# A graph attention layer on one core: the running maximum moves from TensorE to VectorE, the accumulator update one group later, and the end is reordered

## The chip, the core and the metric

The kernel runs on one core of a Trainium2 chip. TensorE (PE) multiplies matrices out of SBUF into PSUM, VectorE (DVE) and ScalarE (ACT) work element by element, GpSimd (POOL) here does nothing but issue indirect gathers, and SyncE (SP) issues the other transfers. The engines run side by side and are ordered by semaphores alone. The metric is the device time of one execution in microseconds. The kernel before takes 2543.44 us (median of three runs, 2543.19 to 2546.44).

## The reference

One message passing layer over 6250 nodes and 206,250 edges that are sorted by their receiver `dst`, all in float32:

```python
h = maximum(layernorm(x), 0)
m = concat(h[src], h[dst], edge_attr)               # 64 + 64 + 32 columns
messages = silu(m @ W1 + b1) @ W2 + b2
att = softmax(silu(m @ Wa1 + ba1) @ Wa2 + ba2)      # over all edges at once
agg = segment_sum(messages * att, dst)
out = x + silu(concat(h, agg) @ Wu1 + bu1) @ Wu2 + bu2
```

The softmax runs over all edges, so the kernel keeps a running maximum and rescales what it has summed whenever the maximum grows.

## The kernel before, in words

**Preparation.** For all nodes the kernel writes two tables to memory: `p_tab`, the part of the two first layers that comes from the source node (128 columns), and `q_tab`, the part from the receiver.

**The groups.** The edges are cut into 81 groups: 80 of 20 tiles of 128 edges, and a last one (number 80, `LAST`) of 12 tiles. Because receivers are sorted, the receivers of a group lie in a window of 96 nodes. Each group is handled in quarters of 4 tiles (five quarters, three in the last group). The loops over groups are written out, so each engine has its own long list of instructions in a fixed order; what sets the order around the change is that hand-written order and the semaphores. The work on one group `g`:

- POOL, `gather`, L396: one indirect DMA per tile reads the 128 rows of `p_tab` into `p_rows`, which has room for two groups. Before quarter `q` of group `g` it waits on `z_ok` until DVE has added quarter `q` of group `g - 2`.
- SP: the receivers as a row copied to 96 partitions (`dst_b`, L281), edge features (L276) and the window of `q_tab` (L271).
- ACT: one-hot columns of the receivers, `comb` (L484, L490).
- PE, `zmm`, L613: `comb` times the window gives `z` in PSUM, one bank per quarter; its last matmul raises `z_done`.
- DVE, `add_rows`, L897: adds the gathered rows to `z`, raises `z_ok`.
- ACT, L516: SiLU of the sum, into `s2`, raises `silu_ok`.
- DVE, `logits`, L884 and L886: attention logits `lg`; L944 adds the bias (`lgb`), L946 takes the maximum along each partition (`pmax`).
- The maximum over partitions goes to PE and back twice: PE transposes `pmax` (`column_max`, L633), DVE takes the maximum of the row (`group_max`, L904), PE multiplies it by a column of ones (`spread_max`, L638), DVE updates the running maximum (`running_max`, L913 and L915) and raises `negm_ok`.
- ACT, `weights`, L504 and L506: the exponentials of the logits and of the change of the maximum (`fade`). `Exp` and `Silu` need different tables, so a table is loaded before each.
- DVE: one-hots of the receivers by edge (`one_hots`, L861), in one buffer `hot`, and the weighted rows `v` (`weighted`, L890 and L891).
- PE, `sums`, L624: 20 tiles of `v` times `hot`, accumulated in PSUM (`ps_part`); the last matmul raises `part_done`.
- DVE, `add_part`, L871 to L876: `acc` = `acc` * `fade` + `ps_part` in the group's window (L874), the maximum that the window was scaled with (`set_ref`, L867), and the sum of the weights (`zp`, L876). L871 reads the window's first node into a register.

The groups overlap. In its part for group `g`, PE does `zmm` of group `g + 1`, with `sums(g - 1)` ahead of the quarters 3 and 4; DVE does the one-hots, weights and `add_part` of group `g - 1` between the quarters of group `g`, and `add_rows` of the first quarter of group `g + 1` just ahead of `add_part`.

**The end.** After the last group DVE updates the maximum, forms `v`, the total weight and its reciprocal (`total_weight`), and adds the last sums (L1006). A branch on `flag` follows, which is taken only when a receiver does not fit its window and everything has to be redone; it is not taken with these inputs. Then `acc` is brought to the common maximum (`rescale`, L1079) and the update layer runs over the nodes in seven blocks: `own_part` (L660) for the node's own features, `aggregate` (L718) for the summed messages, SiLU (L555), `new_rows` (L728), `whole_y` (L1086), and the store.

## Time and profile before

| | |
|---|---|
| median of three runs | 2543.44 us |
| the profiled execution's own time | 2545.81 us |
| its span, first to last instruction | 2544.0 us |
| POOL busy | 1529.6 us (60%), 1628 instructions |
| PE busy (matmuls) | 1335.2 us (52%), 7010 |
| DVE busy | 953.6 us (37%), 1722 |
| ACT busy | 925.1 us (36%), 1106 |
| TensorE's mean granted clock | 0.653 of full speed |
| DMA | mean 90 GB/s |

No engine is busy for more than 60% of the span, and all of them show about the same share in each of the page's 40 slices: the groups repeat with one pattern from about 110 us to 2474 us, and nothing in it is full. So the time has to be looked for in waits. The ends of PE's matmuls in the trace are modelled from their size; what was observed is when they started, and when another engine that waits for their semaphore goes on.

### The profile page before, as it was taken

To read this page: it belongs to the slowest core of one execution; us is meant where nothing else is said; L and a number is where in the kernel's file an instruction comes from. 1 tells how busy PE (TensorE), PEld (TensorE's weight loads), DVE (VectorE), ACT (ScalarE), POOL (GpSimd) and SP (SyncE) were. 2 spreads that over 40 slices of the span, in tenths; PEclk is the share of its full clock that TensorE was granted. 3 is DMA by queue.
4 is the path that set the end of the run, shared out by engine and by line. 5 is a ranking of instruction groups with operands and counts; after the bars stand their busy time and mean duration, and the time that the engine had idled before them with its cause. 6 is when DMAs were issued, how large, how long until landed. Compare 5 with 4: busy or idle time off the path is not lost.

```text
span 2544.0 us, 20784 instructions
## 1 busy us (share of the span) xinstructions
PE 1335.2 (52%) x7010; PEld 1126.5 (44%) x7010; DVE 953.6 (37%) x1722; ACT 925.1 (36%) x1106; POOL 1529.6 (60%) x1628
## 2 busy tenths in 40 slices
PE   5245555555455555555455555555555455555556
PEld 3234444444444444444444444444444444444444
DVE  4234334433333333433333333333333333443345
ACT  3333333433333333343333333343333333333333
POOL 3665656666666656666666666666666665666650
PEclk8666666666766666666766666666766666666667
DMA  7433333333333333333333333333333333333321
GB/s 193 105 88 84 88 85 91 87 88 92 97 88 87 87 85 90 88 88 89 98 90 88 87 86 89 89 87 87 97 93 88 88 87 85 91 87 87 95 67 27
DMA packets 101988, 228.42 MB, mean 90 GB/s; under 512 B 45185, under 2 KB 65461, under 8 KB 91637
## 3 DMA queue, kind: packets, MB, share of 16 engines
q1 hardware_dynamic: 47588, 120.63, 18.2%
q0 software_dynamic: 51584, 105.75, 16.3%
q8 instruction: 58, 0.95, 0.2%
q10 hardware_dynamic: 2704, 0.66, 0.1%
q14 instruction: 54, 0.43, 0.1%
HBM read 218.91 MB, written 8.00 MB: 89 GB/s over the span
## 4 chain that ended last, share of the span: by engine, by line
another core or an unknown queue 53%; ACT 17%; DVE 14%; issue 11%; PE 3%; DVEq 1%; ACTq 0%; SPq 0%; DMA 0%
ACT s L516 5%; DVE bank L897 5%; ACT L516 4%; ACT comb L484 3%; DVE prod L884 3%; ACT comb L490 3%; DVE lg L886 3%; PE bank L624 1%; ACT bank L504 1%; PE bank L613 1%; DVE lgb L944 1%; PE bank L575 1%; DVE gmax L904 1%; ACT fade L506 1%
## 5 line engine op out<-in xcount | busy, mean ns | idle before, releaser
L396 POOL DMA_INDIRECT p_rows<-p_tab,src_all x1612 | 1521.6, 944 | 943.7 <-issue 466.9
L613 PE MATMUL bank<-q_win,comb 128*128 128x128 f32 x3224 | 825.6, 385 | 842.6 <-issue 832.1
L613 PEld LDWEIGHTS bank<-q_win,comb 128*128 128x128 f32 x3224 | 669.0, 279 | 952.2 <-issue 950.9
L516 ACT ACTIVATE s<-bank 128x512 f32<-128x512 f32 x403 | 239.0, 594 | 1434.4 <-DVE bank L897 1424.7
L874 DVE SCALAR_TENSOR_TENSOR acc<-acc,fade,bank 65x96 f32 x80 | 24.8, 310 | 1330.3 <-remote 1326.7
L624 PE MATMUL bank<-hot,v 128*65 128x96 f32 x3224 | 393.7, 300 | 165.2 <-issue 149.7
L624 PEld LDWEIGHTS bank<-hot,v 128*65 128x65 f32 x3224 | 378.4, 180 | 186.0 <-issue 169.0
L897 DVE TENSOR_TENSOR bank<-bank,p_rows 128x512 f32<-128x512 f32 x403 | 277.0, 688 | 15.7 <-issue 15.7
L484 ACT ACTIVATE comb<-dst_b,row_of 96x1024 f32<-96x1024 int32 (+1 forms) x162 | 217.8, 1345 | 55.3 <-DMA dst_b<-dst_row 55.3
L490 ACT ACTIVATE comb<-comb,ones 96x1024 f32<-96x1024 f32 (+1 forms) x162 | 218.8, 1351 | 2.7
L861 DVE TENSOR_TENSOR hot<-bank,rel 128x960 f32<-128x960 f32 x162 | 185.1, 1143 | 0.0
L884 DVE TENSOR_TENSOR prod<-s,bank 128x512 f32<-128x512 f32 (+2 forms) x163 | 130.9, 803 | 134.4 <-ACT s L516 128.3
L886 DVE TENSOR_REDUCE lg<-prod 128x8 f32<-128x512 f32 (+2 forms) x163 | 132.4, 812 | 5.6
L504 ACT ACT_TABLE_LOAD x81 | 103.9, 1283 | 75.7 <-issue 64.4
L891 DVE TENSOR_TENSOR v<-s,bank 128x1300 f32<-128x1300 f32 x80 | 119.9, 1499 | 0.0
L516 ACT ACT_TABLE_LOAD x81 | 103.9, 1283 | 1.4
L633 PE MATMUL bank<-ident,pmax 128*1 128x128 f32 x81 | 29.8, 368 | 99.7 <-issue 96.7
L638 PE MATMUL bank<-gmax,ones 1*128 1x1 f32 x162 | 46.7, 355 | 42.2 <-DVE gmax L904 41.2
L638 PEld LDWEIGHTS bank<-gmax,ones 1*128 1x128 f32 x162 | 39.8, 303 | 64.6 <-DVE gmax L904 64.5
L633 PEld LDWEIGHTS bank<-ident,pmax 128*1 128x1 f32 x81 | 6.4, 79 | 135.3 <-issue 131.5
L904 DVE TENSOR_REDUCE gmax<-bank 1x1 f32<-1x128 f32 x81 | 21.8, 269 | 16.8 <-remote 16.3
L504 ACT ACTIVATE bank<-lgb,neg_max 128x20 f32<-128x20 f32 (+1 forms) x81 | 22.7, 281 | 1.0
(107 smaller groups left out, 321.0 us busy)
## 6 DMA issues: line engine op xcount, KB each, us to landing
dst_b<-dst_row SPq DMA_DIRECT2D x80, 960.0 KB
p_rows<-p_tab,src_all POOLq DMA_INDIRECT x1612
comb<-efT SPq DMA_DIRECT2D x80, 320.0 KB
q_win<-q_tab SPq DMA_DIRECT2D x81, 48.0 KB
p_tab<-s SPq DMA_DIRECT2D x12, 256.0 KB
q_tab<-s SPq DMA_DIRECT2D x12, 256.0 KB
out<-s SPq DMA_DIRECT2D x6, 256.0 KB, 2.3
x_sb<-x SPq DMA_DIRECT2D x2, 512.0 KB, 5.0
```

The lines of the kernel that those rows point to most:

```text
L396: pool.indirect_dma_start(p_rows[:, a, t * H2:(t + 1) * H2], None, p_tab, bass.IndirectOffsetOnAxis(src_all[:, g * TG + t:g * TG + t + 1], ...
L484: nc.scalar.activation(comb[0:WIN, a, c0:c1], dst_b[:, c0:c1], ACT.Abs, bias=row_of[0:WIN, bass.ds(g, 1)]).then_inc(abs_ok, 1)
L490: nc.scalar.activation(comb[0:WIN, a, c0:c1], comb[0:WIN, a, c0:c1], ACT.Relu, scale=-1.0, bias=ones[0:WIN, 0:1]).then_inc(comb_ok, 1)
L504: nc.scalar.activation(ps_w[:, 0:tiles(g)], lgb[:, 0:tiles(g)], ACT.Exp, bias=nm).then_inc(w_ok, 1)
L516: nc.scalar.activation(silu_rows(a, q), halves(ps_z[q][:]), ACT.Silu).then_inc(silu_ok, 1)
L613: last = nc.tensor.matmul(ps_z[q][:, (t % TQ) * H2:(t % TQ + 1) * H2], comb[:, a, t * P:(t + 1) * P], q_win[:, a, :], start=True, stop=True)
L624: last = nc.tensor.matmul(ps_part[0:U1, 0:WIN], v[:, t, :], hot[:, t * WIN:(t + 1) * WIN], start=(t == 0), stop=(t == T - 1))
L861: nc.vector.tensor_tensor(hot[:, t0 * WIN:(t0 + n) * WIN].rearrange("p (t n) -> p t n", t=n), iota_c[:, 0:WIN].unsqueeze(1).broadcast_to([ ...
L884: nc.vector.tensor_tensor(prod[:, 0:t1 - t0], att, wa2c.unsqueeze(1).broadcast_to([P, t1 - t0, U]), ALU.mult).then_inc(s_sem, 1)
L886: nc.vector.tensor_reduce(lg[:, t0:t1], prod[:, 0:t1 - t0], AX.X, ALU.add).then_inc(s_sem, 1)
L891: return nc.vector.tensor_tensor(v[:, 0:T, :], s2[:, ab, 0:T, 0:U1], ps_w[:, 0:T].unsqueeze(2).broadcast_to([P, T, U1]), ALU.mult)
L897: nc.vector.tensor_tensor(ps_z[q][:], ps_z[q][:], p_rows[:, a, q * 512:(q + 1) * 512], ALU.add).then_inc(z_ok, 1)
```

## The change

It has three parts.

**The maximum on VectorE.** PE no longer takes part in it. `biased` writes the biased logits once for all 128 partitions, as before, and then the logits of the partitions 32 to 63, 64 to 95 and 96 to 127 beside each other into the first 32 partitions. `lane_max` takes the maximum along those 32 partitions, the new `spread_max` transposes the 32 values with a 32 by 32 transpose and takes the maximum again, so that each of 32 partitions holds it (`top`), and `running_max` writes the running maximum into four times 32 partitions with four instructions in place of one. The transpose of `bad` that fed `flag` moves into `sums(1)`, and its reader into `add_part(1)`.

**`acc` a group later.** In its part for group `g` DVE now calls `add_part(g - 2)`, after `running_max(g - 1)` and ahead of the one-hots of group `g - 1`; before, it called `add_part(g - 1)` at the end of that part.

**The end.** `add_part(79)` and the one-hots of the last group come after the last maximum; `v` is formed before the sum of the weights; ACT runs a small `Exp` ahead of the last `weights`; PE does three more `own_part` ahead of the last sums and the matmul for the total weight in the middle of them; the branch on `flag` stands ahead of the wait for the last sums and of the addition.

```diff
 def weights(g, a):
-    act.wait_ge(negm_ok, g + 1)
+    act.wait_ge(negm_ok, 4 * (g + 1))
 ...
 groups(act, group)
+nc.scalar.activation(rz[:], ones[:, 0:1], ACT.Exp)
 weights(LAST, 0)
 ...
 def group(g, a):                       # PE
-    if late:
-        column_max(g - 1)
     for q in [q for q in (0,) if q in quarters]:
         zmm(nxt, 1 - a, q)
-    if late:
-        spread_max(g - 1)
     for q in [q for q in (1, 2) if q in quarters]:
         zmm(nxt, 1 - a, q)
     if late:
         sums(g - 1)
 ...
 own_part(0)
 own_part(1)
-column_max(LAST)
-spread_max(LAST)
-pe.wait_ge(zp_ok, 1)
 pe.wait_ge(silu_ok, LAST * NQ + TL // TQ)
-nc.tensor.matmul(ps_zall, ones[:], zp[:], start=True, stop=True).then_inc(zall_done, 1)
-sums(LAST)
+for b in range(2, 5):
+    own_part(b)
+pe.wait_ge(acc_ok, LAST)
+pe.wait_ge(v_ok, NG)
+for t in range(TL):
+    if t in (0, TL // 2):
+        pe.wait_ge(hot_ok, 2 * LAST + 1 + 2 * t // TL)
+    if t == TL // 2 + 2:
+        pe.wait_ge(zp_ok, 1)
+        nc.tensor.matmul(ps_zall, ones[:], zp[:], ...).then_inc(zall_done, 1)
+    last = nc.tensor.matmul(ps_part[0:U1, 0:WIN], v[:, t, :], hot[:, t * WIN:(t + 1) * WIN], ...)
 ...
+def biased(g):                         # DVE from here on
+    T = tiles(g)
+    dve.wait_ge(s_ok, (g + 1) * 4 if g < LAST else g * 4 + T // TQ * 2)
+    nc.vector.tensor_scalar(lgb[:, 0:T], lg[:, 0:T], ba2c[:], None, ALU.add).then_inc(lg_ok, 1)
+    for k in range(1, 4):
+        lanes = slice(32 * k, 32 * (k + 1))
+        nc.vector.tensor_scalar(lgb[0:32, k * T:(k + 1) * T], lg[lanes, 0:T], ba2c[lanes, :], None, ALU.add).then_inc(lg_ok, 1)
+def lane_max(g):
+    T = tiles(g)
+    dve.wait_ge(lg_ok, 4 * (g + 1))
+    nc.vector.tensor_reduce(qmax[:], lgb[0:32, 0:4 * T], AX.X, ALU.max).then_inc(qmax_ok, 1)
+def spread_max(g):
+    dve.wait_ge(qmax_ok, g + 1)
+    nc.vector.transpose(qmaxB[:], qmax[:].broadcast_to([32, 32])).then_inc(qmaxB_ok, 1)
+    dve.wait_ge(qmaxB_ok, g + 1)
+    nc.vector.tensor_reduce(top[:], qmaxB[:], AX.X, ALU.max).then_inc(top_ok, 1)
 ...
 def group(g, a):
-    for q in range(T // TQ):
-        if q + 1 < T // TQ:
-            add_rows(g, a, q + 1)
 ...
-        if q == 0 and late:
-            group_max(g - 1)
-        if q == 1 and late:
-            running_max(g - 1)
-            one_hots(g - 1, 0)
 ...
-    if nxt is not None:
-        add_rows(nxt, 1 - a, 0)
-    if late:
-        add_part(g - 1, 1 - a)
+    add_rows(g, a, 1)
+    if late:
+        spread_max(g - 1)
+    add_rows(g, a, 2)
+    logits(a, 0, 2, silu_ok, g * NQ + 2, s_ok, g * 4)
+    if late:
+        running_max(g - 1)
+    if g > 1:
+        add_part(g - 2, a)
+    if late:
+        one_hots(g - 1, 0)
+    add_rows(g, a, 3)
+    if late:
+        one_hots(g - 1, 1)
+        weighted(g - 1, 1 - a)
+    add_rows(g, a, 4)
+    logits(a, 2, NQ, silu_ok, g * NQ + NQ, s_ok, g * 4 + 2)
+    biased(g)
+    add_rows(nxt, 1 - a, 0)
+    lane_max(g)
```

**DVE in the middle of the run, before.** The rows follow each other from `add_rows` of quarter 0 of the next group (`gath00`) through `add_part` to the next group's first steps. `z_done`, `part_done` and `maxT_done` are raised by PE, `gath..` by the gathers.

```order
L897 TENSOR_TENSOR bank<-bank,p_rows 128x512 [waits gath00,z_done]
L871 TENSOR_LOAD base_i
L871 ISA x2
L874 ISA [waits part_done]
L874 SCALAR_TENSOR_TENSOR acc<-acc,fade,bank 65x96
L867 REGISTER_ALU
L867 TENSOR_SCALAR ref<-ones,neg_max 65x96
L876 SCALAR_TENSOR_TENSOR zp<-zp,fade,wsum 128x1
L897 TENSOR_TENSOR bank<-bank,p_rows 128x512 [waits gath01,z_done]
L904 TENSOR_REDUCE gmax<-bank 1x1 [waits maxT_done]
L897 TENSOR_TENSOR bank<-bank,p_rows 128x512 [waits gath02,z_done]
```

**The same place after the change**, from `add_rows` of quarter 1 to `add_part`:

```order
L897 TENSOR_TENSOR bank<-bank,p_rows 128x512 [waits gath11,z_done]
L917 STREAM_TRANSPOSE qmaxB<-qmax 32x32 [waits qmax_ok]
L919 TENSOR_REDUCE top<-qmaxB 32x1 [waits qmaxB_ok]
L897 TENSOR_TENSOR bank<-bank,p_rows 128x512 [waits gath12,z_done]
L884 TENSOR_TENSOR prod<-s,bank 128x512 [waits s_ok,silu_ok]
L886 TENSOR_REDUCE lg<-prod 128x8 [waits s_ok]
L930 SCALAR_TENSOR_TENSOR neg_max<-top,neg_max 32x1 [waits negm_ok,top_ok]
L930 SCALAR_TENSOR_TENSOR neg_max<-top,neg_max 32x1 x3
L868 TENSOR_LOAD base_i
L868 ISA x2
L874 ISA [waits part_done]
L874 SCALAR_TENSOR_TENSOR acc<-acc,fade,bank 65x96
```

The wait on `part_done` stood behind quarter 0 and ahead of quarter 1. It now stands behind quarters 1 and 2, the first two quarters' logits and the running maximum, ahead of the one-hots and of quarter 3, and it asks for the group before.

**DVE at the end, before**, from the mask on the last weights to the branch on `flag` (L1009, L1010):

```order
L997 TENSOR_TENSOR bank<-bank,mask 128x12 [waits w_ok]
L999 TENSOR_REDUCE wsum<-bank 128x1 [waits wm_ok]
L1001 SCALAR_TENSOR_TENSOR zp<-zp,fade,wsum 128x1 [waits ws_ok]
L1002 TENSOR_TENSOR v<-s,bank 128x780
L976 COPY zall<-bank 128x1 [waits zall_done]
L978 RECIPROCAL rz<-zall 128x1 [waits zall_ok]
L980 TENSOR_SCALAR wws<-ww,rz 65x64 [waits rz_ok]
L1006 REGISTER_ALU [waits part_done]
L1006 SCALAR_TENSOR_TENSOR acc<-acc,fade,bank 65x96
L1009 TENSOR_LOAD flag [waits acc_ok]
L1009 ISA x2
L1010 COMPARE_AND_BRANCH
```

**The end after the change**, from the first half of the last one-hots (L858) to the reading of `flag` for the branch (L1015):

```order
L858 TENSOR_TENSOR hot<-bank,rel 128x576
L864 ISA [waits ref_ok]
L864 TENSOR_SCALAR ref<-ones,neg_max 65x96
L1006 TENSOR_TENSOR bank<-bank,mask 128x12 [waits w_ok]
L1008 TENSOR_TENSOR v<-s,bank 128x780 [waits wm_ok]
L858 TENSOR_TENSOR hot<-bank,rel 128x576
L1010 TENSOR_REDUCE wsum<-bank 128x1
L1012 SCALAR_TENSOR_TENSOR zp<-zp,fade,wsum 128x1 [waits ws_ok]
L983 COPY zall<-bank 128x1 [waits zall_done]
L985 RECIPROCAL rz<-zall 128x1 [waits zall_ok]
L987 TENSOR_SCALAR wws<-ww,rz 65x64 [waits rz_ok]
L1015 TENSOR_LOAD flag
```

`v` (L1002, now L1008) stood behind the sum of the weights and `zp` and stands ahead of them now; the one-hots of the last group moved into the wait for the weights; and the reading of `flag` and the branch, which stood behind the last `part_done`, stand ahead of it (the wait on `part_done` follows the branch).

## Rows read from the trace of the kernel before

**Rows 1.** Page, chain that ended last: shares by engine.

```profile
another core or an unknown queue 53%; ACT 17%; DVE 14%; issue 11%; PE 3%; DVEq 1%; ACTq 0%; SPq 0%; DMA 0%
```

**Rows 2.** Waits of the whole run: who waited for whom, total us, times, longest.

```profile
DVE acc L874 <- remote: 1326.7, 77, 17.4
POOL p_rows L396 <- issue: 466.9, 1532, 0.3
POOL p_rows L396 <- DVE bank L897: 439.6, 79, 8.9
```

**Rows 3.** Timeline of a middle group: start us, us, instruction, idle before.

```profile
1203.46 5.17 PE L624 MATMUL bank<-hot,v 128*65 128x96 f32 x40 [2.08 <-issue]
...
1207.90 0.69 DVE L897 TENSOR_TENSOR bank<-bank,p_rows 128x512 f32<-128x512 f32 x1
...
1225.88 0.31 DVE L874 SCALAR_TENSOR_TENSOR acc<-acc,fade,bank 65x96 f32 x1 [17.29 <-remote]
...
1226.42 0.69 DVE L897 TENSOR_TENSOR bank<-bank,p_rows 128x512 f32<-128x512 f32 x1
...
1227.38 0.94 POOL L396 DMA_INDIRECT p_rows<-p_tab,src_all  x1 [5.41 <-DVE bank L897]
...
1227.85 3.78 PE L613 MATMUL bank<-q_win,comb 128*128 128x128 f32 x16
...
1229.37 1.28 ACT L504 ACT_TABLE_LOAD   x1 [0.84 <-issue]
...
1231.99 1.50 DVE L891 TENSOR_TENSOR v<-s,bank 128x1300 f32<-128x1300 f32 x1
```

**Rows 4.** Windows: one burst of gathers, busy us and count of each engine.

```profile
1227.40:1252.00 24.60, 12.82 (x74) 10.44 (x75) 9.59 (x15) 10.79 (x13) 18.81 (x20) 0.71 0.39 101
```

**Rows 5.** Timeline where the gathers end: last gather, last but one groups.

```profile
2470.55 5.24 PE L624 MATMUL bank<-hot,v 128*65 128x96 f32 x40 [1.91 <-issue]
...
2473.12 0.95 POOL L396 DMA_INDIRECT p_rows<-p_tab,src_all  x1 [0.30 <-issue]
...
2476.21 0.31 DVE L874 SCALAR_TENSOR_TENSOR acc<-acc,fade,bank 65x96 f32 x1 [0.52 <-PE bank L624]
...
2489.62 0.31 DVE L874 SCALAR_TENSOR_TENSOR acc<-acc,fade,bank 65x96 f32 x1 [1.08 <-PE bank L624]
```

**Rows 6.** Timeline of the first group, engines PE, DVE and POOL.

```profile
120.82 0.27 PE L633 MATMUL bank<-ident,pmax 128*1 128x128 f32 x1
...
142.76 0.28 DVE L904 TENSOR_REDUCE gmax<-bank 1x1 f32<-1x128 f32 x1 [16.26 <-remote]
...
143.91 0.94 POOL L396 DMA_INDIRECT p_rows<-p_tab,src_all  x1 [5.50 <-DVE bank L897]
```

**Rows 7.** Lines by form: busy us, mean ns of one, idle before.

```profile
L861 DVE TENSOR_TENSOR hot<-bank,rel 128x960 f32<-128x960 f32 x160 | 183.7, 1148 | 0.0
L915 DVE SCALAR_TENSOR_TENSOR neg_max<-bank,neg_max 128x1 f32<-128x1 f32 x80 | 11.9, 149 | 1.1 <-PE bank L638 1.1
L944 DVE TENSOR_SCALAR lgb<-lg,ba2c 128x20 f32<-128x20 f32 x80 | 19.1, 239 | 2.8
```

**Rows 8.** Timeline of the end: last group's sums and first rescale.

```profile
2500.00 0.31 DVE L874 SCALAR_TENSOR_TENSOR acc<-acc,fade,bank 65x96 f32 x1 [2.08 <-PE bank L624]
...
2500.54 1.41 DVE L861 TENSOR_TENSOR hot<-bank,rel 128x576 f32<-128x576 f32 x2
...
2506.26 1.28 ACT L504 ACT_TABLE_LOAD   x1 [3.08 <-DVE neg_max L915]
...
2508.63 0.96 DVE L1002 TENSOR_TENSOR v<-s,bank 128x780 f32<-128x780 f32 x1
...
2513.88 0.31 DVE L1006 SCALAR_TENSOR_TENSOR acc<-acc,fade,bank 65x96 f32 x1 [3.73 <-PE bank L624]
...
2517.82 3.49 DVE L1079 TENSOR_TENSOR acc<-acc,ref 65x1024 f32<-65x1024 f32 x3 [3.63 <-issue]
...
2521.00 2.08 PE L660 MATMUL bank<-hP,wu1d 128*128 128x512 f32 x2
```

More of the change, by code:

```diff
@@ L184, in build @@
         (row_ok, rel_ok, hot_ok, abs_ok, comb_ok) = (sem(n) for n in ("row_ok", "rel_ok", "hot_ok", "abs_ok", "comb_ok"))
-        (z_done, z_ok, silu_ok, s_ok, lg_ok, pmax_ok, maxT_done, gmax_ok, maxB_done, negm_ok) = (
-            sem(n) for n in ("z_done", "z_ok", "silu_ok", "s_ok", "lg_ok", "pmax_ok", "maxT_done",
-                             "gmax_ok", "maxB_done", "negm_ok"))
+        (z_done, z_ok, silu_ok, s_ok, lg_ok, qmax_ok, qmaxB_ok, top_ok, negm_ok) = (
+            sem(n) for n in ("z_done", "z_ok", "silu_ok", "s_ok", "lg_ok", "qmax_ok", "qmaxB_ok", "top_ok", "negm_ok"))
         (w_ok, wm_ok, v_ok, part_done, acc_ok, ref_ok) = (
@@ L622, in sums @@
                 T = tiles(g)
+                if g == 1:
+                    pe.wait_ge(bad_ok, 1)
+                    nc.tensor.transpose(ps_part[0:1, P:2 * P], bad[:, 2:3], ident[:])
                 for t in range(T):
@@ L625, in sums @@
                 last.then_inc(part_done, 1)
-            def column_max(g):
-                pe.wait_ge(pmax_ok, g + 1)
-                if g == 1:
-                    pe.wait_ge(bad_ok, 1)
-                    nc.tensor.transpose(ps_small[0:1, P:2 * P], bad[:, 2:3], ident[:])
-                nc.tensor.transpose(ps_small[0:1, 0:P], pmax[:], ident[:]).then_inc(maxT_done, 1)
-            def spread_max(g):
-                pe.wait_ge(gmax_ok, g + 1)
-                nc.tensor.matmul(ps_small[:, 0:1], ones[0:1, :], gmax[:], start=True, stop=True).then_inc(maxB_done, 1)
             def group(g, a):
@@ L666, in _ @@
             own_part(1)
-            column_max(LAST)
-            spread_max(LAST)
-            pe.wait_ge(zp_ok, 1)
             pe.wait_ge(silu_ok, LAST * NQ + TL // TQ)
-            nc.tensor.matmul(ps_zall, ones[:], zp[:], start=True, stop=True).then_inc(zall_done, 1)
-            sums(LAST)
+            for b in range(2, 5):
[7 more added lines that the diff above has]
+                    pe.wait_ge(zp_ok, 1)
+                    nc.tensor.matmul(ps_zall, ones[:], zp[:], start=True, stop=True).then_inc(zall_done, 1)
+                last = nc.tensor.matmul(ps_part[0:U1, 0:WIN], v[:, t, :], hot[:, t * WIN:(t + 1) * WIN], start=(t == 0), stop=(t == TL - 1))
+            last.then_inc(part_done, 1)
             pe.wait_ge(flag_ok, 1)
@@ L707, in _ @@
                 nc.tensor.matmul(ps_zall, ones[:], zp[:], start=True, stop=True).then_inc(g_zall, 1)
+                own_part(2)
+                own_part(3)
                 pe.wait_ge(g_scale, 1)
@@ L729, in new_rows @@
                 last.then_inc(y_done, 1)
-            own_part(2)
             for b in range(UB + 1):
                 aggregate(b)
-                if 3 + b <= UB:
-                    own_part(3 + b)
+                if b < 2:
+                    own_part(5 + b)
                 if b > 0:
@@ new lines, in running_max @@
+            def running_max(g):
+                dve.wait_ge(top_ok, g + 1)
+                wait(dve, negm_ok, 4 * g)
+                for k in range(4):
+                    nm = neg_max[32 * k:32 * (k + 1), bass.ds(g, 1)]
+                    if g == 0:
+                        nc.vector.tensor_scalar(nm, top[:], -1.0, None, ALU.mult).then_inc(negm_ok, 1)
+                    else:
+                        nc.vector.scalar_tensor_tensor(nm, top[:], -1.0, neg_max[0:32, bass.ds(g - 1, 1)], ALU.mult, ALU.min).then_inc(negm_ok, 1)
@@ L923, in group @@
             def group(g, a):
-                nxt = following(g)[0]
-                late = not (isinstance(g, int) and g == 0)
-                T = tiles(g)
-                for q in range(T // TQ):
-                    if q + 1 < T // TQ:
-                        add_rows(g, a, q + 1)
-                    if q == 2 and late:
-                        one_hots(g - 1, 1)
-                    if q == 1:
-                        logits(a, 0, 2, silu_ok, g * NQ + 2, s_ok, g * 4)
-                    if q == T // TQ - 1:
-                        logits(a, 2, T // TQ, silu_ok, g * NQ + T // TQ, s_ok, g * 4 + 2)
-                    if q == 0 and late:
-                        group_max(g - 1)
-                    if q == 1 and late:
-                        running_max(g - 1)
-                        one_hots(g - 1, 0)
-                    if q == 2 and late:
-                        weighted(g - 1, 1 - a)
@@ L943, in group @@
[L943 to L950 removed]
+                nxt = g + 1
+                late = g > 0
@@ L1072, in _ @@
                 nc.vector.memset(ref[:], 1.0).then_inc(g_acc0, 1)
-                dve.wait_ge(g_acc0, 4)
+                nc.vector.memset(fade[:, 0:1], 1.0).then_inc(g_acc0, 1)
+                nc.vector.memset(ps_part[0:U1, 0:WIN], 0.0).then_inc(g_acc0, 1)
+                dve.wait_ge(g_acc0, 6)
+            dve.wait_ge(part_done, NG)
+            win = acc[:, bass.ds(node, WIN)]
+            nc.vector.scalar_tensor_tensor(win, win, fade[0:U1, 0:1], ps_part[0:U1, 0:WIN], ALU.mult, ALU.add).then_inc(acc_ok, 1)
+            dve.wait_ge(acc_ok, NG)
             def rescale(b):
```

61 lines of the change are left out of this document (23 added, 38 removed).

## The prediction

> **What bounds the kernel now.** I read the busy shares first: no engine is above 60%, so time is lost in waits. Next the chain that ended last: 53% of the span is a release that the profile cannot match [rows 1]. Since one core runs, "another core" can only mean an engine here whose signal is not where its record ends. The waits name the place: VectorE (DVE) stands 1326.7 us, in 77 of 80 groups, ahead of L874, the update of `acc`, which waits for `part_done` from TensorE (PE) [rows 2].
>
> The timeline shows what is odd. PE's 40 matmuls of `sums` start at 1203.46 and last 5.17 us, so by their rows they end at 1208.6. DVE has nothing left to do after 1208.6, yet L874 starts at 1225.88 [rows 3]. The row's end is no proof, for PE's ends are modelled. By the Trainium skill (Perfetto Trace Analysis, Per-instruction lifecycle: what the profiler-reported window actually captures) the end of a TensorE row is an estimate, and the semaphore comes later; it names no gap of 17 us. The wait is the same whichever PE signal is due: in the first group it is `maxT_done`, raised by the transpose at 120.82, seen by L904 at 142.76 [rows 6].
>
> So PE's signals are held back. Until when? POOL gathers in bursts. One burst is 20 gathers, each 0.944 us (the window has 18.81 us for 20, which cuts one off) plus 0.305 us of issue (466.9 / 1532) [rows 2, 4], 1.249 us together, 25.0 us a group. Then POOL stops, because `p_rows` is full and DVE has added nothing. It stopped at 1227.38 - 5.41 = 1221.97, and the signal came 3.9 us later; in the first group it stopped at 138.41 and L904 went on 4.35 us later [rows 3, 6]. And once the last gather is over (2473.12) the wait is gone: `sums` start at 2470.55, last 5.24, and L874 starts at 2476.21 after 0.52 us of waiting; the next group takes 2489.62 - 2476.21 = 13.4 us instead of 30.1 [rows 5]. My reading: while gathers run, PE's completions are prompt only for some time after a stop, then late, and they all come 3.9 us after POOL has stopped. The stop frees PE, PE frees DVE, DVE frees POOL. One cycle is 20 x 1.249 + 5.41 - 0.305 = 30.1 us, and 1225.88 - 30.1 = 1195.8 is the release before, so `sums` ended 12.8 us after a release and were late. A signal soon after a release is prompt: L915, which needs PE's L638, waited 1.1 us in all 80 groups [rows 7].
>
> POOL's 5.1 us of extra idle per cycle (5.41 - 0.305) is thus what a group could lose, not DVE's 17.3 us.
>
> **The change part by part.** Durations are from the profiled execution, whose own time is 2545.8 us (span 2544.0); the median of the runs is 2.4 us less.
>
> *Maximum on DVE.* Gone are a transpose, a matmul and L904. Added per group are three more additions like L944 (0.24 us each), a transpose and a reduction, and three more L915 (0.15 us each) [rows 7], about 1.2 us plus the 32 by 32 transpose. That transpose has no row. Between the smallest DVE row here (0.15) and one with 20 times the elements (L861's 1.15) I take 0.3 us. DVE is busy for 9.59 of 24.6 us [rows 4], so 1.5 us a group is hidden by its wait; uncovered it would be 80 x 1.5 = 120 us, which I carry as the upper end, 0 as the lower (no gain below that: outside the held-back stretch L915 waited for PE only 1.1 us in the whole run [rows 7]). Three of these additions are SBUF to SBUF. In the rows L944 runs 80 times, and the gathers' issue gap never exceeds 0.3 us [rows 2]: price 0. By the Trainium skill (SBUF — State Buffer, Who interferes with whom) a tensor_scalar between SBUF tiles can take the port pair that GpSimd needs to write descriptors; by that rule the sum would grow by at most 240 x 0.24 = 57 us, and the gap row speaks against it.
>
> *`acc` a group later.* DVE no longer stops behind quarter 0. It goes on through quarters 1 and 2, the logits and the running maximum, to the wait for the sums of the group before. Three things follow.
> (a) `negm_ok` is raised ahead of the wait, so ACT's table load (1.28 us at 1229.37), exponentials and most of the rest happen in it. After a release DVE does `add_part` (0.54 us from L874 to L897), one-hots 1.15, quarter 3 0.69, one-hots 1.15, the sum of weights and `v` (1.50): `v` is ready 5.2 us after the release. Before it took 1231.99 + 1.50 - 1225.88 = 7.6 us [rows 3, 7]. `sums` so end at about 10.4 us, not 12.8.
> (b) POOL restarts later where DVE was held ahead of `add_part`: 0.54 + 1.15 + 0.69 + 0.27 = 2.65 us after the release against 1227.38 - 1225.88 = 1.50, that is 1.15 us more. Where DVE is held ahead of an `add_rows` instead, it restarts 0.54 us sooner.
> (c) If `part_done` comes within the prompt stretch, DVE passes it and consumes quarters 3, 4, 0 of the next group until another signal is late, so POOL makes more than 20 gathers per stop.
> The mean idle per stop becomes 5.1 + (1.15 - 0.54) / 2 = 5.4 us. With K quarters per stop a group takes 25.0 + 5.4 x 5 / K. K is 5 now. Its bounds are 5 (nothing gained) and 10, what `p_rows` holds. The prompt stretch ends somewhere between 3 us and 12.8 us after a release; 10.4 us lies near its late end, so I expect `part_done` to pass in some cycles and quarter 3 and 4's matmuls behind it to be caught. I take K = 6, the value nearest to the row of today: 29.5 us, 0.6 us less per group, 79 x 0.61 = 48 us.
>
> *The end.* The wait of 2.08 us for `part_done` ahead of 2500.00, `add_part` (0.54) and the last one-hots (1.41) leave the way to the last maximum: 4.0 us. The table load of 1.28 us [rows 8] goes into ACT's idle 3.08 us, and 0.35 us of sum and `zp` move behind `v`: 1.6 us. The branch, 3.63 us behind L1006, moves into the 3.73 us for the sums: 3.6 us, all covered unless those get shorter. Three `own_part` (2.08 us each) move ahead of the sums, where PE waits; PE is then the engine to wait for, but DVE and ACT follow it closely, so 0 to 6 us, I take 3. The last maximum's own path I take as equal on both sides: 1.5 us of additions here against a trip to PE and back there. Sum 12 us, bounds 8 and 16.
>
> Together 2545.8 - 48 - 12 = 2485.8, in runs of the median 2483.4.
>
> **Rivals.**
> *A. One stop per group, later each time: slower.* If `sums` at 10.4 us are still late, then DVE is held ahead of `add_part` in every group, having consumed exactly 5 quarters, and (b) alone remains: 79 x 1.15 = 91 us, less 12: 2543.4 + 79 = 2622. It decides as soon as the prompt stretch is shorter than 10.4 us. For it: the transpose of the first group, issued at 120.82, was late too, 17.6 us before the gathers stopped at 138.41 [rows 6]. Against: the late mode must begin in a gap of 2.4 us to let this happen, or earlier.
> *B. The gathers alone bound it.* If the late signals are no longer needed at all because everything is a group late, POOL never stops: 25.0 us a group, 79 x 5.1 = 403 us, less 12: 2128. For it: DVE, ACT and PE need 13.4 us for a group [rows 5]. Against: DVE still needs `z_done` of quarters 3 and 4 and of the next quarter 0, which come from the same PE queue behind `sums`, and those signals were just as late. The Trainium skill says in the same page (Identifying the Most-Contended Engine) to judge by the busiest engine; that is POOL, and by it this rival would be the forecast.
> *C. Nothing but the end.* The lag of (b) and a few quarters gained by (c) cancel (K = 5.3): 2543.4 - 12 = 2531, with 5 us to either side.
>
> **How the numbers follow.** Forecast 0.45 (K from 5.6 to 8, that is 2425 to 2518 with the end's bounds), A 0.29, B 0.13, C 0.13. The time is the forecast's, 2484. The range of 8 in 10 goes from 2400 to 2624: it takes in the forecast, A and C, and leaves out B and a DVE path that shows uncovered. About 0.2%, 5 us, is what runs of this kernel can tell from no change. Faster: 0.45 + 0.13 + 0.10 of C = 0.68. Within 0.2%: 0.03 of C and 0.02 of A, 0.05. Slower: the rest of A, 0.27.
>
> **What would show it.** In the profile after: POOL's waits for L897 should be fewer than 79, about 65, with about 5.7 us each (5.4 and the usual issue gap); the count is K. DVE's unmatched waits should be spread over L874 and L897 instead of L874 alone. If L874 still has nearly 80 of them and POOL waits 6.5 us, it is A; if POOL's waits for DVE are gone and its share nears 75%, it is B. `v` should end about 5 us after the release. From the end of the gathers to the last instruction, 70 us now, it should be about 58. The forecast is wrong at its root if waits of some 17 us remain while POOL is not gathering, or if PE's signals come late long after POOL has stopped.

## The result: 2.7% slower, by one longer stop of POOL per group

| | before | after |
|---|---|---|
| median of four runs | 2543.32 us | 2612.59 us (2605.69 to 2620.04) |
| ratio | 1 | 1.027, 95% interval 1.0241 to 1.0300 |
| span of the profiled execution | 2544.0 us | 2611.2 us |
| POOL's waits for an `add_rows` | 439.6 us, 79 times | 491.6 us, 80 times |

The forecast was 2484 us, faster, with a range of 2400 to 2624; the kernel became slower. It did what rival A said (2622 us). The trace of the changed kernel, first the waits (who waited for whom, total us, times, longest), which answer to [rows 2]:

```profile
DVE acc L874 <- remote: 1306.8, 75, 28.4
...
POOL p_rows L398 <- DVE bank L897: 491.6, 80, 8.3
POOL p_rows L398 <- issue: 466.8, 1531, 0.3
```

DVE still stands ahead of L874 in nearly every group, and POOL waits 6.15 us each time (491.6 / 80) where it waited 5.56 (439.6 / 79). The gathers' issue gap is what it was. Two middle groups of the changed kernel, as [rows 3] show one of before:

```profile
1195.16 0.31 DVE L874 SCALAR_TENSOR_TENSOR acc<-acc,fade,bank 65x96 f32 x1 [17.50 <-remote]
...
1200.07 4.84 PE L630 MATMUL bank<-hot,v 128*65 128x96 f32 x40 [1.52 <-DVE v L891]
...
1226.25 0.31 DVE L874 SCALAR_TENSOR_TENSOR acc<-acc,fade,bank 65x96 f32 x1 [17.52 <-remote]
...
1226.38 1.15 ACT L486 ACTIVATE comb<-dst_b,row_of 96x1024 f32<-96x1024 int32 x1 [15.76 <-remote]
...
1226.79 1.15 DVE L858 TENSOR_TENSOR hot<-bank,rel 128x960 f32<-128x960 f32 x1
...
1227.86 0.69 DVE L897 TENSOR_TENSOR bank<-bank,p_rows 128x512 f32<-128x512 f32 x1
...
1228.81 0.95 POOL L398 DMA_INDIRECT p_rows<-p_tab,src_all  x1 [6.38 <-DVE bank L897]
...
1229.60 1.50 DVE L891 TENSOR_TENSOR v<-s,bank 128x1300 f32<-128x1300 f32 x1
...
1231.15 6.31 PE L630 MATMUL bank<-hot,v 128*65 128x96 f32 x40 [1.92 <-DVE v L891]
...
1257.31 0.31 DVE L874 SCALAR_TENSOR_TENSOR acc<-acc,fade,bank 65x96 f32 x1 [17.49 <-remote]
```

POOL stopped at 1228.81 - 6.38 = 1222.43; L874 went on 3.82 us later, as before (3.91). But then came `add_part`, the first one-hots (1.15) and only then quarter 3, and POOL restarted 2.56 us after the release, not 1.50. `v` ends at 1231.10, 4.85 us after the release (5.2 forecast, 7.6 before). The sums start on it and end, by their rows, at 1237.46, 11.2 us after the release; their signal is late and is seen only by the L874 of 1257.31. In the group before, they ran from 1200.07 to 1204.91, at a granted clock of 0.72 in place of 0.54, and ended 9.75 us after the release of 1195.16: they were late too. ACT's L486, which waits for TensorE's `z_done`, goes on 0.13 us after L874: the delay is not one of DVE alone. Two rows far apart give the period, the time from one group to the next; of before:

```profile
320.72 0.31 DVE L874 SCALAR_TENSOR_TENSOR acc<-acc,fade,bank 65x96 f32 x1 [17.24 <-remote]
...
2462.89 0.31 DVE L874 SCALAR_TENSOR_TENSOR acc<-acc,fade,bank 65x96 f32 x1 [17.27 <-remote]
```

and after:

```profile
324.90 0.31 DVE L874 SCALAR_TENSOR_TENSOR acc<-acc,fade,bank 65x96 f32 x1 [17.48 <-remote]
...
2531.18 0.31 DVE L874 SCALAR_TENSOR_TENSOR acc<-acc,fade,bank 65x96 f32 x1 [17.41 <-remote]
```

Between the two rows lie 71 groups: 30.17 us each before, 31.07 after. That makes 71 x 0.90 = 64.1 of the 67.2 us between the spans. The first of these rows is 4.2 us later, and from the last to the end are 80.0 us in place of 81.1.

The first groups of the changed kernel went another way:

```profile
171.26 0.31 DVE L874 SCALAR_TENSOR_TENSOR acc<-acc,fade,bank 65x96 f32 x1 [1.44 <-remote]
...
190.05 0.31 DVE L874 SCALAR_TENSOR_TENSOR acc<-acc,fade,bank 65x96 f32 x1
...
220.61 0.31 DVE L874 SCALAR_TENSOR_TENSOR acc<-acc,fade,bank 65x96 f32 x1
...
262.72 0.31 DVE L874 SCALAR_TENSOR_TENSOR acc<-acc,fade,bank 65x96 f32 x1 [28.42 <-remote]
```

Twice the sums of the group before were in time and L874 did not wait; DVE was held ahead of quarters instead, and POOL stopped after 44, 4, 24, 4 and 32 gathers. From 262.72 on, every stop comes after exactly 20 gathers.

The end kept almost nothing of its forecast 12 us. Windows from the first `rescale` (in the changed kernel from the last addition, 0.4 us ahead of it) to the last instruction, before and after (busy us and count of PE, PEld, DVE, ACT and POOL, then PE's granted clock, DMA share, GB/s):

```profile
2517.80:2544.00 26.20, 20.92 (x84) 10.36 (x84) 11.44 (x14) 4.48 (x7) 0.00 (x0) 0.76 0.28 62
```

```profile
2576.90:2611.20 34.30, 27.54 (x80) 14.07 (x80) 11.68 (x15) 5.37 (x8) 0.00 (x0) 0.52 0.21 48
```

The update layer takes 34.3 us in place of 26.2, with four matmuls fewer, at a granted clock of 0.52 in place of 0.76: the forecast had not priced the clock.

### The profile page after: what moved, and what is told of

The parts are those of the page before. It is cut to its first block, busy times and chain, and to the rows that moved or that the text cites. A ratio compares the mean times of both kernels' runs of the same rounds, so it can differ in the third digit from the quotient of the medians.

```text
span 2611.2 us, 20946 instructions
## 1 busy us (share of the span) xinstructions
PE 1193.7 (46%) x6767; PEld 1038.0 (40%) x6767; DVE 1067.0 (41%) x2289; ACT 942.7 (36%) x1107; POOL 1534.3 (59%) x1628
## 4 chain that ended last, share of the span: by engine, by line
another core or an unknown queue 51%; DVE 28%; issue 15%; PE 3%; ACT 2%; DVEq 2%; ACTq 0%
DVE bank L897 6%; DVE prod L884 5%; DVE v L891 4%; DVE hot L858 3%; DVE lg L886 3%; DVE lgb L906 2%; DVEq L868 1%; ACT s L518 1%; DVE neg_max L930 1%; PE bank L578 1%; DVE qmax L912 1%; PE bank L726 0%; PE bank L716 0%; DVE qmaxB L917 0%
## 5 line engine op out<-in xcount | busy, mean ns | idle before, releaser
L398 POOL DMA_INDIRECT p_rows<-p_tab,src_all x1612 | 1526.3, 947 | 992.4 <-DVE bank L897 491.6
L616 PE MATMUL bank<-q_win,comb 128*128 128x128 f32 x3224 | 742.1, 355 | 1168.1 <-issue 1132.0
L616 PEld LDWEIGHTS bank<-q_win,comb 128*128 128x128 f32 x3224 | 621.1, 259 | 1273.4 <-issue 1269.7
L486 ACT ACTIVATE comb<-dst_b,row_of 96x1024 f32<-96x1024 int32 (+1 forms) x162 | 219.0, 1352 | 1239.8 <-remote 1023.6
L874 DVE SCALAR_TENSOR_TENSOR acc<-acc,fade,bank 65x96 f32 x80 | 24.8, 310 | 1307.6 <-remote 1306.8
L630 PE MATMUL bank<-hot,v 128*65 128x96 f32 x3200 | 399.4, 302 | 197.0 <-DVE v L891 150.9
L858 DVE TENSOR_TENSOR hot<-bank,rel 128x960 f32<-128x960 f32 x162 | 184.7, 1141 | 0.0
L906 DVE TENSOR_SCALAR lgb<-lg,ba2c 32x20 f32<-32x20 f32 (+1 forms) x243 | 55.0, 226 | 9.2 <-issue 1.4
L930 DVE SCALAR_TENSOR_TENSOR neg_max<-top,neg_max 32x1 f32<-32x1 f32 x320 | 46.9, 147 | 7.6
L903 DVE TENSOR_SCALAR lgb<-lg,ba2c 128x20 f32<-128x20 f32 (+1 forms) x81 | 31.8, 393 | 2.9
L508 ACT ACTIVATE fade<-neg_max 128x1 f32<-128x1 f32 x80 | 22.4, 280 | 0.0
L864 DVE TENSOR_SCALAR ref<-ones,neg_max 65x96 f32 x81 | 21.1, 260 | 0.6 <-issue 0.6
```

Of the source, the lines that this page charges most:

```text
L398: pool.indirect_dma_start(p_rows[:, a, t * H2:(t + 1) * H2], None, p_tab, bass.IndirectOffsetOnAxis(src_all[:, g * TG + t:g * TG + t + 1], ...
L486: nc.scalar.activation(comb[0:WIN, a, c0:c1], dst_b[:, c0:c1], ACT.Abs, bias=row_of[0:WIN, bass.ds(g, 1)]).then_inc(abs_ok, 1)
L616: last = nc.tensor.matmul(ps_z[q][:, (t % TQ) * H2:(t % TQ + 1) * H2], comb[:, a, t * P:(t + 1) * P], q_win[:, a, :], start=True, stop=True)
L630: last = nc.tensor.matmul(ps_part[0:U1, 0:WIN], v[:, t, :], hot[:, t * WIN:(t + 1) * WIN], start=(t == 0), stop=(t == T - 1))
L858: nc.vector.tensor_tensor(hot[:, t0 * WIN:(t0 + n) * WIN].rearrange("p (t n) -> p t n", t=n), iota_c[:, 0:WIN].unsqueeze(1).broadcast_to([ ...
```

## The experiments

All but one of the 18 runs met something that the first runs did not show: the kernel before took 2107 to 2108 us on the chips they ran on, and their traces show no late signal of TensorE (a "late signal" is a semaphore that a waiter sees long after the matmul that raises it). Each is compared with the kernel before on its own chip.

**1. Parts undone or moved, after the model of the prediction.** `e1_acc_back` (its last line stands in `last_group`):

```diff
-                if g > 1:
-                    add_part(g - 2, a)
 ...
                 lane_max(g)
+                if late:
+                    add_part(g - 1, 1 - a)
 ...
-                add_part(g - 2, a)
```

> The changed kernel with one part undone: add_part(g - 1) stands at the end of the group's part again, behind add_rows of the next group's quarter 0. The maximum on VectorE and the new end stay. Theory 1 (rival A of the prediction): TensorE's signals come once per group, 3.9 us after POOL's gathers stop, and the period is 25.0 us plus POOL's stop, which ends when DVE has added a quarter. DVE then restarts POOL 1.50 us after the release as in the kernel before, so the period falls from 31.07 to about 30.1 us: 2612.6 - 79 x 0.95 = 2537 us, a little below the kernel before. Theory 2 (the added work of the maximum on VectorE is what costs, by 1.5 us a group or by slowing the gathers): the time stays near 2610 us, POOL's mean for a gather or its issue gap is longer than in the kernel before.

`e2_rows3_next`:

```diff
                     add_part(g - 2, a)
+                add_rows(g, a, 3)
                 if late:
                     one_hots(g - 1, 0)
-                add_rows(g, a, 3)
```

> The changed kernel with add_rows of quarter 3 moved directly behind add_part, ahead of both one-hots (1.15 us less between the release and POOL's restart). Theory 1: POOL's stop is 5.2 us instead of 6.35, the period 29.9 us: 2612.6 - 79 x 1.15 = 2522 us. The one-hots and v come 0.7 us later, which costs nothing because the sums are late anyway. Theory 3 (the period is set by TensorE's own backlog, not by POOL's stop): no change, 2610 us; or slower by up to 55 us since v is 0.7 us later.

`e3_rows3_ahead`:

```diff
+                add_rows(g, a, 3)
                 if g > 1:
                     add_part(g - 2, a)
```

> The changed kernel with add_rows of quarter 3 ahead of add_part's wait for part_done. DVE is then held at quarter 3, whose z_done comes behind part_done on TensorE, and at the release POOL is restarted after 0.69 + 0.27 = 0.96 us. Theory 1: POOL's stop is about 4.8 us, the period 29.5 us: 2612.6 - 79 x 1.6 = 2486 us. Theory 3 (TensorE's backlog sets the period): no gain.

`e4_pool_waits`:

```diff
                         pool.wait_ge(z_ok, (g - 2) * NQ + q + 1)
+                    if g > 3 and q == 2:
+                        pool.wait_ge(part_done, g - 3)
```

> The changed kernel, but POOL waits itself for part_done of three groups before, ahead of its quarter 2, that is one quarter earlier than where it runs out of room. Nothing else is changed. Theory 1: the signals come 3.9 us after this stop, wherever in the burst it is, and POOL goes on at once, with a free quarter in hand, without waiting for DVE. Period 25.0 - 0.3 + 3.9 = 28.6 us: 2612.6 - 79 x 2.5 = 2415 us. DVE's wait at add_part falls from 17.5 us by some 5 us. Theory 4 (the signals come a fixed time after something else, such as the start of the gathers or of the load of dst_b): POOL's stop grows by the 5.0 us by which it is earlier, and the time is that of the changed kernel or slower, 2612 to 2700 us.

Measured: 2109.9, 2109.1, 2110.1 and 2108.0 us, the kernel before 2107.8 us (31 runs) on the same chip; ratios 1.0008, 1.0007, 1.0008 and 1.0005, each with 1 inside its interval. None of the expected sizes appeared, because the late signals did not. These runs tell nothing of theories 1 to 4, only that with prompt signals none of the edits shows.

**2. The two kernels unchanged, and e4 again.** No edit.

> The kernel before, unchanged, with its own trace on the chip of this call. In the four runs of the first experiments it took 2107.8 us instead of 2543.4. Theory 5: on some chips or at some times TensorE's signals are not held back, POOL never stops, and a group takes the 25.0 us of its 20 gathers; the trace then shows no wait of DVE at L874 and POOL busy for some 73%. Where they are held back, the trace is that of before, 2543 us.

> The changed kernel, unchanged. Where the kernel before takes 2108 us, all edits of the groups are hidden behind POOL's gathers, so only the way from the last gather to the end counts: theory of the prediction's end, 2108 - 12 = 2096 us if TensorE's clock is the same there; as the four first experiments, which all have the new end, came within 2 us of the kernel before, I rather expect 2108 +- 5 us, the gain of the end given back by a slower clock or a later branch. Where the kernel before takes 2543 us: 2612 us as measured.

> The changed kernel with POOL's own wait for part_done ahead of quarter 2. Where signals are held back (before at 2543 us): 2415 us by theory 1, at least 2612 us by theory 4. Where they are not (before at 2108 us): 2108 us again, since part_done is early.

Measured on another chip: before 2108.0, changed 2108.0 (1.0005, 0.9991 to 1.0019), e4 2110.7 (1.0014, 1.0001 to 1.0028). The trace of before there, waits:

```profile
POOL p_rows L396 <- issue: 489.9, 1608, 0.3
...
DVE acc L874 <- PE bank L624: 3.1, 1, 3.1
```

and the chain that ended last:

```profile
POOL 71%; issue 23%; PE 3%; DMA 1%; DVE 1%; ACTq 0%; ACT 0%; POOLq 0%; DVEq 0%; SPq 0%
```

L874 is released by its true releaser, once in the whole run with a wait, POOL does not stop between groups, and a group takes its 20 gathers, 24.9 us. This is the mechanism of rival B, reached by the state of the chip and not by the edit. By the Trainium skill (Perfetto Trace Analysis, Identifying the Most-Contended Engine) the engine to look at is the busiest one. That is POOL in both traces: here its 20 gathers are the whole period, in the trace of before they are 25.0 of 30.2 us. The traces differ in one more thing: that of the kernel before at 2544 us holds 9117 semaphore events, 306 of the 404 of `z_done` among them; this one holds 34,068, with all 404. Both hold the event of every `part_done`: it comes 0.26 us after the start of the last matmul of `sums` here, and 12.3 to 19.1 us after it in the first 77 groups at 2544 us. Late signals and missing events stand together in all three traces of that state; what makes either is not shown.

**3. The late signal made by hand.** Since the delay could not be called up, it was built in: POOL writes an unused buffer where it ran out of room, and DVE waits for that. These runs therefore test what a delay of that length does to each order, not where the delay comes from. `h1_held_before` (kernel before):

```diff
+        held = sem("held")
+        idle = sb("idle", [P, 4096])
 ...
+                        if q == 1 and 4 <= g <= 80:
+                            nc.gpsimd.memset(idle[:], 0.0).then_inc(held, 1)
                         pool.wait_ge(z_ok, (g - 2) * NQ + q + 1)
 ...
                 dve.wait_ge(part_done, g + 1)
+                if g <= 76:
+                    dve.wait_ge(held, g + 1)
```

> The kernel before with the late signal made by hand: at the place where POOL ran out of room in the trace of before (ahead of quarter 1 of group g, g from 4), POOL now writes an unused buffer for about 3.6 us and only then raises a semaphore held, and add_part waits for it beside part_done. So part_done is passed some 3.9 us after the last gather, as in the trace of before, whatever TensorE does. The result is the same. Theory 1 (the period is the gathers plus POOL's stop, and the stop is 3.9 us plus DVE's way to the next add_rows): 25.0 - 0.3 + 3.9 + 1.5 = 30.1 us a group, 2108 + 77 x 5.1 = 2500 us, and POOL waits about 5.4 us in 77 groups. Theory 6 (TensorE's slowness itself made the period, not the stop): some us less per group.

`h2_held_after` is the same in the changed kernel, with `q == 3`, g to 79 and `g <= 75`.

> The changed kernel with the same late signal made by hand, at the place where POOL ran out of room in its trace (ahead of quarter 3, g from 4 to 79). Theory 1: DVE's way from the release to add_rows is 2.65 us, the period 31.2 us, 2108 + 76 x 6.2 = 2579 us, so 78 us slower than the same with the order of before. If DVE's order is not what made the changed kernel slower, both kernels with the late signal made by hand take the same time.

`h3_held_rows3_next` is h2 with the move of e2.

> As the run before it, with add_rows of quarter 3 directly behind add_part. Theory 1: DVE's way is 1.50 us again, the period 30.1 us, 2108 + 76 x 5.1 = 2496 us: moving one instruction takes the whole loss back. Otherwise it stays with the changed order, near 2579 us.

`h4_held_pool_goes_on` is h2 with `q == 2`.

> The changed kernel with the late signal made by hand, but raised one quarter earlier (ahead of quarter 2), where POOL still has a free quarter. POOL then goes on by itself while DVE does add_part, one-hots and add_rows. Theory 1: the stop is the 3.6 us alone, 25.0 - 0.3 + 3.9 = 28.6 us a group, 2107 + 76 x 3.6 = 2381 us, 197 us less than the same signal one quarter later. If the stop is always followed by DVE's way, it stays near 2578 us.

| | expected | measured | ratio to before, interval |
|---|---|---|---|
| h1, order of before | 2500 | 2510.0 us | 1.1912, 1.1880 to 1.1944 |
| h2, changed order | 2579 | 2578.1 us | 1.2240, 1.2211 to 1.2268 |
| h3, quarter 3 behind `add_part` | 2496 | 2498.2 us | 1.1858, 1.1830 to 1.1887 |
| h4, signal one quarter earlier | 2381 | 2380.9 us | 1.1299, 1.1278 to 1.1321 |

h2 over h1 is 2578.1 / 2510.0 = 1.027, the ratio of the first result. h3 keeps the maximum on VectorE and has the period of h1, 29.9 us: with the delay made by hand the maximum costs nothing that shows, and moving one instruction takes the whole loss back. The stop in h1, from the timeline (start us, us, instruction, idle before):

```profile
1197.95 3.53 POOL L397 MEMSET idle<- 128x4096 f32 x1
...
1201.70 0.31 DVE L880 SCALAR_TENSOR_TENSOR acc<-acc,fade,bank 65x96 f32 x1 [17.11 <-POOL idle L397]
...
1202.25 0.69 DVE L903 TENSOR_TENSOR bank<-bank,p_rows 128x512 f32<-128x512 f32 x1
...
1203.21 0.95 POOL L400 DMA_INDIRECT p_rows<-p_tab,src_all  x1 [1.72 <-DVE bank L903]
```

in h2:

```profile
1210.38 3.52 POOL L399 MEMSET idle<- 128x4096 f32 x1
...
1214.13 0.31 DVE L880 SCALAR_TENSOR_TENSOR acc<-acc,fade,bank 65x96 f32 x1 [17.41 <-POOL idle L399]
...
1215.73 0.69 DVE L903 TENSOR_TENSOR bank<-bank,p_rows 128x512 f32<-128x512 f32 x1
...
1216.69 0.95 POOL L402 DMA_INDIRECT p_rows<-p_tab,src_all  x1 [2.78 <-DVE bank L903]
```

and in h3:

```profile
1205.10 3.53 POOL L399 MEMSET idle<- 128x4096 f32 x1
...
1208.84 0.31 DVE L880 SCALAR_TENSOR_TENSOR acc<-acc,fade,bank 65x96 f32 x1 [16.43 <-POOL idle L399]
...
1209.39 0.69 DVE L903 TENSOR_TENSOR bank<-bank,p_rows 128x512 f32<-128x512 f32 x1
...
1210.34 0.95 POOL L402 DMA_INDIRECT p_rows<-p_tab,src_all  x1 [1.72 <-DVE bank L903]
```

From the end of the buffer's write POOL waits 1.72 us in h1 and h3, and 2.78 us in h2: the 1.06 us are the one-hots between `add_part` and `add_rows`. In h4 POOL does not wait for DVE:

```profile
POOL p_rows L402 <- DVE bank L903: 22.5, 74, 0.3
```

74 waits of 0.3 us are the issue gap. The stop is the signal's delay plus DVE's way to the next `add_rows`, and the second term goes away where POOL has a free quarter left at the time of the signal. Theory 6 is out but for a small rest: TensorE was not slow in these runs, and the periods are 29.9 us in h1 and 31.0 in h2, where the first result had 30.2 and 31.1.

**4. The end.** `e5_own_part_back`:

```diff
-            for b in range(2, 5):
-                own_part(b)
 ...
+            own_part(2)
             for b in range(UB + 1):
                 aggregate(b)
-                if b < 2:
-                    own_part(5 + b)
+                if 3 + b <= UB:
+                    own_part(3 + b)
```

> The changed kernel with own_part 2 to 6 again where they stood before, between the aggregates of the update layer; the rest of the new end stays. Both kernels need 49.8 us from the last gather to the end in the traces taken at 2108 us: the changed one has the common maximum applied 5.5 us sooner, and loses 5.4 us in the update layer, which it runs at a granted clock of 0.5 to the end, where before had 1.0 in the last 13 us. Theory 7 (with own_part between the aggregates TensorE has fewer gaps and gets the clock back): 5 us less than the changed kernel, 44.5 us from the last gather to the end. Theory 8 (the clock is granted by other things, and the added 4 instructions of 2.08 us count): the same or up to 4 us slower.

Measured: 2103.4 us against 2107.1, ratio 0.9982 (0.9968 to 0.9996). From the end of the last gather (2058.60) to the last instruction are 43.1 us. Windows of that stretch in e5, cut at the addition of the last sums and where PE's matmuls get short:

```profile
2058.60:2075.40 16.80, 11.16 (x63) 8.79 (x61) 8.67 (x31) 10.64 (x14) 0.01 (x1) 0.79 0.03 6
2075.40:2086.30 10.90, 9.28 (x20) 3.43 (x20) 3.80 (x4) 1.37 (x2) 0.00 (x0) 0.53 0.01 2
2086.30:2101.70 15.40, 11.37 (x65) 6.77 (x64) 7.95 (x11) 3.11 (x5) 0.00 (x0) 0.93 0.46 104
```

and in the changed kernel on its 2108 us chip:

```profile
2054.60:2070.10 15.50, 10.11 (x67) 7.21 (x65) 8.70 (x31) 9.56 (x14) 0.01 (x1) 0.94 0.02 6
2070.10:2085.80 15.70, 12.47 (x32) 5.27 (x32) 5.58 (x6) 3.13 (x4) 0.00 (x0) 0.50 0.08 19
2085.80:2104.40 18.60, 15.08 (x49) 8.81 (x48) 6.07 (x9) 2.42 (x4) 0.00 (x0) 0.50 0.32 72
```

There are four matmuls of `own_part` more in the stretch behind the addition, and it takes 26.3 us in place of 34.3; the granted clock is 0.93 in its last 15 us, 0.50 to the end otherwise. From the last gather to the end the changed kernel takes 49.8 us, 6.7 more than e5. That is what theory 7 said.

**5. A version meant to beat both,** `f1_rows3_and_own_part`: the edits of e2 and e5 together.

> A version meant to beat both kernels: the changed one with add_rows of quarter 3 directly behind add_part and with own_part 2 to 6 where they stood before. Where the kernel before takes 2107 us: 2103 us as measured with own_part alone, since the place of add_rows costs nothing there. Where it takes 2543 us (TensorE's signals late): 2612 - 91 - 8 = 2513 us.

> The changed kernel with add_rows of quarter 3 directly behind add_part and own_part back in its place, where signals are late: POOL's stop is 1.15 us shorter than with the changed kernel, 2612 - 79 x 1.15 - 8 = 2513 us, some 30 us below the kernel before. Rival: the group is bound by TensorE's slow stretch itself and nothing is gained, 2604 us. Without late signals: 2103 us.

2103.9 us against 2106.8 (0.9982, 0.9970 to 0.9994; five rounds) on one chip, 2102.5 against 2107.0 (0.9981, 0.9965 to 0.9996) on another. It is 0.2% below the kernel before where signals are prompt, a small difference, but the interval leaves out 1 on both chips. Where they are late it was not measured.

**6. What calls the late signals up.** `p1_more_signals`, on the kernel before:

```diff
+        tick = sem("tick")
 ...
+                    if (t + 1) % TQ:
+                        last.then_inc(tick, 1)
                 last.then_inc(z_done, 1)
 ...
+                    if t < T - 1:
+                        last.then_inc(tick, 1)
                 last.then_inc(part_done, 1)
```

> The kernel before, in which every matmul of zmm and of sums raises a semaphore that nobody waits for: 39 to 40 signals of TensorE per group in place of 7. Theory 9 (TensorE's signals were late in the first runs because the signals of the gathers, 16 for each of 20 gathers a group, and TensorE's share a path that was full): more signals bring the late state back, DVE stands 17 us ahead of L874 and the time goes toward 2500 us, at least some tens of us above 2107. Otherwise the time stays at 2107 us, and what made the signals late lay outside of the kernel.

Measured: 2537.3 us, but the kernel before, run between these, took 2522.5 us (ratio 1.0064, 1.0041 to 1.0087). The late signals were there for both, and in the first result without any added ones, so these are not what it takes; they cost 0.6% where signals are late. The edit makes 42 signals a group out of 8 (the expectation says 39 to 40 out of 7). The waits of p1:

```profile
DVE acc L879 <- remote: 1302.1, 76, 17.3
...
POOL p_rows L397 <- DVE bank L902: 426.1, 79, 10.1
```

It is the picture of [rows 2] again, and its trace again holds few events (11,109). It was the chip on which experiment 2, h1 to h3 and e5 had found 2107 to 2108 us: the state comes and goes. On another chip the kernel before was at 2107.0 us again. There ran e4 and e1 as above, and `n1_no_dst_b`, the changed kernel without `load_dst_b` for the groups from 2 on.

> The changed kernel with POOL's own wait for part_done ahead of quarter 2, once more, since the last run met the late signals again (the kernel before at 2522 us there). With late signals, theory 1: the signals come 3.9 us after this stop, POOL goes on at once, 28.6 us a group, 2415 us if the changed kernel takes 2612 there, less by the 20 us by which the kernel before was faster there. Theory 4 (the signals do not depend on where POOL stops): 2590 us or more. Without late signals: 2108 us.

> The changed kernel with add_part(g - 1) back at the end of the group's part. With late signals, theory 1: period 30.1 us as in the kernel before, 2612 - 79 x 0.95 = 2537 us, that is the later update of acc is what cost, and the maximum on VectorE nothing. Theory 2 (the maximum on VectorE costs): near 2600 us. Without late signals: 2110 us.

> The changed kernel without the load of dst_b for the groups from 2 on (ACT makes its one-hots from the stale receivers, so z and the result are other numbers; the instructions are the same). With late signals: if the load of 960 KB beside the sums is what makes TensorE late, part_done comes in time in most groups and the time falls toward 2108 us; if only the running gathers do, it stays near 2600 us. Without late signals: 2108 us.

Measured: 2108.3 (1.0006), 2107.7 (0.9999) and 2109.9 us (1.0020, 1.0004 to 1.0035), the values named for prompt signals. They decide nothing on the late ones.

## Why the prediction was wrong

**The reading of before** held: POOL's stop sets the period, some 3.9 us to the signal plus DVE's way. It was right on the first result, and the runs with the signal made by hand came within 10 us of its sums. What it did not see is that the delay belongs to a state that comes and goes: the same kernel takes 2107 us without it. The row "another core or an unknown queue 53%" [rows 1] was the only sign; in the trace with complete events this share is gone.

**Maximum on DVE** was hidden, as forecast. The transpose took 0.189 us (0.3 taken), the three small additions 0.226 each; the gathers' mean went from 0.944 to 0.947 us, 1612 x 0.003 = 5 us at most. By the Trainium skill (SBUF — State Buffer, Who interferes with whom) DVE and GpSimd share a port pair, and while one holds it the other is blocked. The gathers paid nothing near the 57 us that the prediction weighed by it. The rule itself is not refuted: the addition over 128 partitions, the same instruction before and after, took 0.410 us (median) in place of 0.235, so it may be DVE that waited. No run isolates that.

**(a)** was right: `v` 4.85 us after the release (5.2). **(b)** was right: 2.56 us to the restart (2.65); h2 and h3 show that the order alone makes it. **(c) is the step that failed.** "I take K = 6": from 262.72 us on, every stop follows 20 gathers, which is K = 5, and there were 80 waits where about 65 were expected. In the trace of before the end of the prompt stretch was bounded only by 3 and 12.8 us after the release, and I placed it beyond 10.4 for no row. Sums that ended 9.75 us after it were late. The mechanism of (c) did occur, in the first groups alone, and won little: the three groups from 171.26 to 262.72 took 91.5 us, the same three before 93.7. Why the kernel then fell into one stop per group is not shown.

With K = 5 the sum of the prediction is its rival A, 2622 us, 9 us above the measured 2612.6, and two misses nearly cancel in that. The stops of the regular groups are 6.37 us on average (72 of them) against 5.51 (73), 0.86 longer in place of 1.15: DVE's way grew from 1.56 to 2.58 us, but the signal came after 3.79 us in place of 3.95. With the gathers' 20 x 0.003 us that is about the 0.90 us a group of the rows above, about 20 us less in all than rival A took. Against that stand 11 us which the end did not give. One more sum is off: with K from 5.6 to 8 the prediction's own formula gives 2391 to 2513 us, not 2425 to 2518.

**The end** was right on the branch and the waits and wrong on the sum: 12 us forecast, 1.1 measured. From the addition of group 76 to `acc` (2462.89 before, 2531.18 after) to the first `rescale` are 46.1 us in place of 54.9, so 8.8 us came in, where the forecast had 9.2 without the `own_part`; the update layer then lost 7.7. In the two traces at 2108 us the last gather to the end takes 49.8 us in the changed kernel and 49.9 in the one before: 5.5 us came in up to `rescale`, and 5.4 went out again in the update layer at half clock. The range from 0 to 6 us for the moved `own_part` weighed their 2.08 us each and not what their absence does to the clock. The sign that the prediction named, 58 us from the end of the gathers in place of 70, did not come either: it was 84, because the last gather of the changed kernel ended 3.7 us before a release and that of the kernel before 11.2 us after one.

Left open: what makes TensorE's signals late (the 18 runs met it once, and no edit was shown to bring it), and what ends the prompt stretch (n1, e4 and e1 did not meet the state). One rival was not tried: every run has a granted clock on record, so none was made without recording, and whether the recording takes part in the delay and in the loss of events cannot be told. That the later `acc` alone carried the loss is shown with the signal made by hand; for the real signal it rests on the trace, where the longer stops make up 64 of the 67 us.

## What to carry to other kernels

Where a producer refills a ring that a consumer empties, and both stop once per round, the round costs the fixed delay plus whatever stands in the consumer between the release and the first slot it frees: put the instruction that frees a slot first, and let the producer reach the wait with a slot in hand. A wait that no row explains is a property to be measured on a second chip before edits are priced on it. Price work moved out of TensorE's gaps also by the clock that the stage loses, read from the granted clock of its window.
